# Swapping the operands of a graph layer's degree count: 49 columns stationary, 128 moving

## The reference, cut to what matters

```
mask = (src != dst)                       # an edge from a node to itself doesn't count
deg  = segment_sum([mask, ones(N)], [dst, arange(N)], num_segments=N)
dinv = where(deg > 0, rsqrt(deg), 0)
out  = segment_sum((dinv[src] * dinv[dst] * mask)[:, None] * (xn @ W)[dst], src)
```

## Time and profile before

| | |
|---|---|
| median of 3 runs | 2781.3 us (2778.11 to 2783.08) |
| the profiled execution: its own time | 2780.86 us |
| its span from the first to the last instruction | 2779.1 us |
| PE, PEld, DVE, ACT, POOL busy | 2278.5, 1817.1, 1423.6, 1216.6, 1320.9 us |
| histogram's products (L1391) | 784 pairs, 84.1 us of MATMUL records |
| end of the projection stage (last product, L1405) | 440.84 us |

### The profile page before, as it was taken

How to read it: one execution, slowest core, us unless ns; L and a number is a source line. 1 busy time by engine, 2 the same in 40 slices (tenths; PEclk the granted TensorE clock), 3 DMA queues, 4 the chain that set the end, 5 groups by cost and what they waited for, 6 DMA issues and landing times.

```text
span 2779.1 us, 53503 instructions
## 1 busy us (share of the span) xinstructions
PE 2278.5 (82%) x12218; PEld 1817.1 (65%) x12219; DVE 1423.6 (51%) x2463; ACT 1216.6 (44%) x3290; POOL 1320.9 (48%) x1388
## 2 busy tenths in 40 slices
PE   1699993888888888888888887748999999999990
PEld 0477773666666666666666644626999999999980
DVE  7699996555555555555555545653222222222225
ACT  2344441665656556565655543631333333333320
POOL 6556564766666666666666653001222222222220
PEclk9799996999999999999999998557999999999995
DMA  4000003333333333333333476240111111111118
GB/s 127 1 1 1 1 1 110 102 94 94 96 94 96 93 96 94 95 96 94 96 93 95 144 151 64 74 131 21 35 36 34 36 34 34 34 34 34 34 29 280
DMA packets 113671, 202.42 MB, mean 73 GB/s; under 512 B 27819, under 2 KB 76195, under 8 KB 113638
## 3 DMA queue, kind: packets, MB, share of 16 engines
q0 software_dynamic: 59232, 143.39, 19.2%
q1 hardware_dynamic: 54406, 58.65, 6.5%
HBM read 167.96 MB, written 33.99 MB: 73 GB/s over the span
## 4 chain that ended last, share of the span: by engine, by line
PE 40%; DVE 30%; DVEq 14%; issue 10%; DMA 3%; POOL 2%; ACT 0%; SPq 0%; ACTq 0%; POOLq 0%
DVE ACC L568 20%; PE B L1577 14%; PE B L1566 14%; DVEq L568 4%; PE B L1452 4%; DVEq L686 3%; DVEq L797 3%; DVE BIG L681 3%; DMA BIG<-table,W2A 2%; PE B L1530 1%; DVEq L807 1%; PE B L1358 1%; PE B L1391 1%; DVE W1A L1110 1%; POOL W2A L504 1%
## 5 line engine op out<-in xcount | busy, mean ns | idle before, releaser
L528 POOL DMA_INDIRECT BIG<-table,W2A x880 | 831.6, 945 | 418.7 <-issue 220.4
L568 DVE TENSOR_TENSOR ACC<-ACC,B 128x512 f32 x880 | 604.8, 687 | 530.4 <-issue 318.4
L1452 PE MATMUL B<-BIG 128*128 128x256 f32 x1760 | 437.4, 393 | 121.6 <-DVE ACC L568 94.2
L1452 PE MATMUL B<-BIG,W2A 128*128 128x256 f32 x1760 | 431.7, 389 | 102.5 <-DVE ACC L568 91.6
L1128 ACT ACTIVATE BIG<-B,SMALL 128x128 f32<-128x128 f32 (+1 forms) x889 | 250.5, 387 | 549.1 <-PE B L1566 549.1
L1452 PEld LDWEIGHTS B<-BIG 128*128 128x128 f32 x1760 | 321.0, 192 | 241.0 <-issue 188.5
L1452 PEld LDWEIGHTS B<-BIG,W2A 128*128 128x128 f32 x1760 | 316.8, 190 | 202.8 <-issue 161.1
L1566 PEld LDWEIGHTS B<-BIG 128*128 128x128 f32 x3360 | 393.1, 193 | 8.0 <-DVE BIG L1080 2.7
L1566 PE MATMUL B<-BIG 128*128 128x128 f32 x3360 | 393.8, 276 | 2.1 <-DVE BIG L1080 2.1
L1577 PE MATMUL B<-W2A,BIG 128*128 x1680 | 390.7, 386 | 0.0
L1577 PEld LDWEIGHTS B<-W2A,BIG 128*128 128x128 f32 x1680 | 310.8, 190 | 50.3
(11 more groups left out here) (224 smaller groups left out, 2343.5 us busy)
## 6 DMA issues: line engine op xcount, KB each, us to landing
BIG<-table,W2A POOLq DMA_INDIRECT x880, 2.7
W1A<-in_w SPq DMA_DIRECT2D x8, 1024.0 KB, 7.5
W2A<-in_w SPq DMA_DIRECT2D x1, 8192.0 KB, 31.5
table<-ACC SPq DMA_DIRECT2D x7, 896.0 KB, 7.1
token_x<-BIG SPq DMA_DIRECT2D x49, 128.0 KB, 1.7
W2A<-in_x SPq DMA_DIRECT2D x1, 6144.0 KB
W1A<-pick_y SPq DMA_DIRECT2D x4, 896.0 KB, 11.3
W2A<-pick_y SPq DMA_DIRECT2D x4, 896.0 KB, 11.5
```

What stands on the lines that cost most here:

```text
L528: pool.indirect_dma_start(G[h][:, u, :], None, table, bass.IndirectOffsetOnAxis(ap=idx_s[h][:, u:u + 1], axis=0)).then_inc(gath[h][u // 2] ...
L568: return dve.tensor_tensor(o, a, b, op)
L1452: last = mm(B[u][:, k * D:(k + 1) * D], OH[h % 2][:, u, k * P:(k + 1) * P], G[h][:, u, :], start=True, stop=True)
```

## The change

Each product of the histogram takes `oh_hi` (49 columns) as the stationary operand and `oh_lo` (128 columns) as the moving one, so that the sum stands in `B[5]` as 49 rows of 128 columns. At the end DVE copies it to SBUF (`hist_rows`, in the place of `xn`, which is no longer needed), PE transposes it back into columns 256 to 304 of the same bank, and DVE adds 1 from there. Two semaphores are new. The one-hots, their layout and their stride stay as they were.

```
+        hist_rows = BIG[0:NT, 2048:2048 + P]
...
             dve.wait_ge(sums_done, 1)
+            dve.tensor_copy(hist_rows, B[5][0:NT, 0:P]).then_inc(hist_out, 1)
             dve.wait_ge(cgroup_T, 1)
...
-            ch.link(ts(col[9][:, 0:NT], B[5][:, 0:NT], 1.0, ALU.add))
+            dve.wait_ge(hist_T, 1)
+            ch.link(ts(col[9][:, 0:NT], B[5][:, 256:256 + NT], 1.0, ALU.add))
...
-            mm(B[5][:, 0:NT], zb[:, 0:P], zb[:, 0:NT], start=True, stop=False)
+            mm(B[5][0:NT, 0:P], zb[:, 0:NT], zb[:, 0:P], start=True, stop=False)
...
-                    last = mm(B[5][:, 0:NT], oh_lo[s][:, :, b], oh_hi[s][:, :, b], start=False, stop=False)
+                    last = mm(B[5][0:NT, 0:P], oh_hi[s][:, :, b], oh_lo[s][:, :, b], start=False, stop=False)
...
-            mm(B[5][:, 0:NT], zb[:, 0:P], zb[:, 0:NT], start=False, stop=True).then_inc(sums_done, 1)
+            mm(B[5][0:NT, 0:P], zb[:, 0:NT], zb[:, 0:P], start=False, stop=True).then_inc(sums_done, 1)
+            pe.wait_ge(hist_out, 1)
+            nc.tensor.transpose(B[5][:, 256:256 + NT], hist_rows, ident[0:NT, 0:NT]).then_inc(hist_T, 1)
 
             pe.wait_ge(cgroup_ready, 1)
             nc.tensor.transpose(B[6][0:CG, 128:256], col[10][:, 0:CG], ident).then_inc(cgroup_T, 1)
```

More of the change, by code:

```diff
@@ L309, in gps_layer @@
         sums_done = sem("sums_done")
+        hist_out, hist_T = sem("hist_out"), sem("hist_T")
         stage_ready, scat = sem("stage_ready"), [sem("scat0"), sem("scat1")]
```

## The result

The changed kernel takes 2965.8 us (median), the kernel before 2782.2 us in the same comparison: a ratio of 1.066, 95% interval 1.0639 to 1.0681. It is slower, as forecast, but by 184 us where 112 were forecast, and outside the range of 2844 to 2912 us. One of its four executions took 12391 us, for a cause that no view here shows, and is left aside; the other three took 2964.4 to 2966.9 us. The profiled execution has a span of 2965.1 us, 186.0 more than before.

What follows compares the result with a forecast made beforehand. It took PE and DVE, both close to their limit in the projection stage, to bound the kernel. 109.0 + 4.1 - 1.5 + 0.8 = +112.4 us on 2780.9 us gave 2893 us, range 2844 to 2912 us.

Steps and rivals of the forecast that it cites:

- What bounds the kernel: Projection stage: PE and DVE both near their limit; PE has almost no slack, and what the stage loses, the kernel loses.
- The swapped products: Histogram on PE: 784 pairs go from 0.097 to 0.236 us, set by strided moving columns, loads hidden; +109.0 us.
- A change of width: PE at the histogram: entering a narrower stationary operand costs 0.09 us, 45 times, counted one way; +4.1 us.
- The end of the sum: End of the stage: DVE's copy from PSUM, PE's transpose and two handovers join the path; +0.8 us.
- What the delay swallows: Projection tiles with histogram: about 9.3 us each, so PE no longer waits for one-hots, and scatters stay hidden; -1.5 us.
- a falling clock: Projection stage: sign of a wrong forecast, granted clock falling to 1.2 GHz and lengthening the projection's 5.36 us too.
- Rival D: Histogram on PE: the narrow load no longer hides, adding 0.097 us a pair; +76 us more, 2969 us; chance 7%.

Runs made afterwards that it cites:

- run 7: The kernel before with its 49 moving columns read side by side, the 128 stationary ones still strided (degrees wrong): 2778.3 us, ratio 0.999.
- run 3: The kernel before with the 128 low digits as both operands, 128 strided columns stationary and 128 moving (degrees wrong): 2965.1 us, ratio 1.065.
- run 4: The kernel before with each histogram product made twice in a row and the sum halved: 2923.1 us, ratio 1.0504.
- run 5: The changed kernel with a tile's 16 swapped products in four parts of four at four places of the tile: 2925.6 us, ratio 1.0524.
- run 6: The changed kernel with both operands read side by side and each product made four times (degrees wrong): 2878.7 us, ratio 1.0355.
- run 1: The changed kernel with its 128 moving columns read side by side instead of 32 bytes apart (degrees wrong): 2782.9 us, ratio 0.9995.
- run 2: The changed kernel with its 49 stationary columns read side by side, the 128 moving ones still strided (degrees wrong): 2962.2 us, ratio 1.0645.
- run 8: The changed kernel with a tile's 16 swapped products in two parts of eight, after keys and values and at tile's end: 2894.9 us, ratio 1.0405.

## Why the prediction was wrong

**What bounds the kernel:** right. Run 7 shows the 2.9 us by which a faster PE brings the stage's end forward, runs 3 to 6 that work added on PE lengthens the kernel.

**The swapped products:** right, mechanism and size. 0.236 us forecast, (3.96 - 0.413)/15 = 0.236 measured; the price is the stride of the moving operand (runs 1 and 2), at either clock: the first histogram of the changed kernel runs at 1.2 GHz and takes the same 3.9 us. In sum 784 x (0.236 - 0.097) = 109 us. One point of the argument was thinner than it looked: the 0.097 of before is the stream's, but the load may be not far behind (at most 0.060, run 7).

**A change of width:** right. L1379's start to L1395's is 307.14 - 306.08 = 1.06 us, where L1375's to L1391's was 0.96 (two starts of the timeline before, 210.85 and 211.81 us): 0.10 against 0.09 forecast. The 0.99 of the second tile shown answers to the 0.89 of such a tile before (325.67 and 326.56 us).

**The end of the sum:** right, 0.74 against 0.8. It doesn't show in the span, which grew by no more than the stage's end moved; 0.74 us is less than the 2.5 us by which the three executions differ.

**What the delay swallows: here it failed.** The step took the 5.36 us of a tile's projection as given and only added the longer histogram to it, "about 9.3 us". PE's waits did go, but the projection lengthened: in 42 of 44 tiles the clock is down behind the histogram, the keys and values pay for it, and the mean tile takes 11.10 us. The stage's end moved by 626.93 - 440.84 = 186.1 us; 109 for the products, 4.5 for the width and -1.5 for the waits leave 74 us, and run 8 gives 71 by itself. The prediction named a falling clock as what would make it wrong but gave it neither a price nor a chance, and so it stood in no rival and not in the range. Rival D came out near the measured time (2969 us) by a mechanism that the trace excludes: it wanted starts over 0.3 us apart and they are 0.236, and in run 2 a shorter load changes next to nothing. That closeness is chance.

The trace of before held the warning. Rows 5 show a histogram of 1.66 us in which the array gets 49 columns per 0.097 us; the same scarcity, 128 per 0.236 us, was forecast to last 3.8. And the first histogram stood in a stretch at 1.2 GHz after a wait of 24.9 us for one-hots, with the projection behind it slow as well. It even held the fall itself, once, in the middle of the stage:

```profile
318.20 1.73 PE L1391 MATMUL B<-W1A 128*128 128x49 bf16 x16 [0.51 <-DVE W1A L568]
...
320.18 3.14 PE L1358 MATMUL B<-BIG 128*128 128x512 f32 x4
```

Behind a wait of 0.51 us and a histogram of 1.73 the keys and values take 3.14 us instead of 1.98, and the granted clock between 320.5 and 324 us is 0.55. I read a PE that is busy by its records as one that keeps its clock. The runs show what went before a fall instead: not a narrow operand (run 3), not length alone (run 6), not the share in the tile (run 5), but an unbroken stretch in which columns come slowly. Counted by tiles, the keys and values run slow in 42 of 44 in the changed kernel and in 39, 36 and 42 in runs 2, 3 and 4; in runs 1, 5, 6 and 8 in 1 (the first tile), 0, 0 and 2. A wait just ahead of the histogram adds to such a stretch: in run 7 six tiles are slow besides the first, each behind a wait of PE of 1.0 to 2.9 us. That the clock follows the stretch is shown; by what rule it does is not.

The Trainium skill (TensorE: Matmul & The Clock Gate, section HAM oscillation — how this bites in real kernels) ties such a fall to gaps in which PE does nothing. The trace of the changed kernel goes further: PE has no such gap in the stage (507.33 of 509 us busy, no wait for one-hots after the first), and the clock falls all the same.

## What to carry to other kernels

Price a matmul's operands by their layout, not by their column counts alone: columns that lie 28 or 32 bytes apart cost the moving side 1.8 to 2.0 ns each at either clock here, where contiguous ones cost 0.42 at 2.4 GHz, so the longer operand should not be the strided moving one. Before lengthening a stretch of such products, look at what else runs on PE at full clock around it: 16 slow products in one piece in each tile cost 109 us of their own and over 70 in their neighbours, and the same 16 in two pieces little more than the 109 (113.5 us in all). And where two engines are even, as PE and DVE are here, bound the gain by the other engine first: no histogram on PE, however cheap, could win more than some 3 us while DVE makes its one-hots as it does.

## What the hardware showed that was not expected

The narrow strided load is dearer than the wide one. With the stream out of the way, a pair with 49 strided stationary columns takes 0.097 us (run 1), with 128 of them at most 0.060 (run 7), and with 49 lying side by side at most 0.056 (run 6). The Trainium skill (TensorE: Matmul & The Clock Gate, section Weight-path perf modes) has the fast load for 128 columns of a type other than f32 only; these runs agree with that, though they don't show the mode itself.

PE's busy time doesn't tell the clock that it is granted: 99.7% busy with a clock of 0.80 in the changed kernel, 99.8% and 0.98 in run 5, 98.3% and 0.98 before.
